# The two later layer norms of a fused attention, state-space and feed-forward kernel: constant in the root's bias, rows normalised, turned and copied in two halves

## The chip, the cores and the metric

One core of a Trainium2 chip runs the whole program in one launch. The metric is the device time of one execution in microseconds (us), lower is better. The engines are PE (TensorE, matmuls and transposes), DVE (VectorE), ACT (ScalarE), POOL (GpSimd) and SP (SyncE, which here only issues transfers). Each runs its own queue in order, and they meet in semaphores.

## What is computed

The input x has 128 rows of 512 numbers, the context 2048 rows of 512. The reference ends in three residual steps:

```
x = x + cross_attention(layernorm(x), ctx, Wq, Wk, Wv, Wo)        # 32 heads, 4 key/value heads
x = x + mamba2(layernorm(x), in_proj, conv, dt_bias, A_log, D, norm_w, out_proj)
x = x + sparse_ffn(layernorm(x), c1, c2, w1, w2)
layernorm(x) = (x - mean(x)) / sqrt(var(x) + 1e-5)                 # over the 512 numbers of a row
```

The second and third layer norm are the ones that the change touches. The first stays as it is.

## The kernel before

The 128 rows lie on the 128 partitions. `res` [128, 512] holds x and takes each residual. The three steps of the reference are three stages that follow one another without overlap in their main data: attention from about 10 to 363 us of the profiled span, the state-space stage from 367 to 586, the feed-forward stage from 590 to the end. Between two stages stands a layer norm, and nothing of the next stage can start before it, since every product reads its result.

A layer norm passes work between three engines. DVE (`norm(k)`) computes statistics of `res` (`bn_stats`, `bn_aggr` into `mean_var`), adds the constant EPS to the variance, ACT (`norm_sqrt`) takes the root, DVE takes the reciprocal and writes `normed` = (res - mean) * rstd over all 512 columns. PE (`norm_transpose`) turns four 128x128 blocks of `normed` into one PSUM bank, bank 7, and ACT (`norm_evac`) copies that bank into `norm_t` [128, 4, 128]. One semaphore, `ln`, counts these 8 steps; each step waits for the count of the one before it. Ahead of the turns PE runs 12 products of the identity (WARM) into bank 5, which nobody reads.

What stands behind each of the two norms:

- Behind the second norm (k = 1), PE makes the product with `w_dt` (4 steps c over 128 rows of the contraction, line 1769) and then the first projections (`in_proj`, line 1780, a loop over 8 chunks of weights, each 16 products). ACT, behind `norm_evac(1, 7)`, takes an exponential (line 891), which needs another function table than the root. DVE, behind `norm(1)`, fills `upper`, reduces five small selector tiles from the identity (`pick`), waits for the product with `w_dt`, and computes the step sizes in a chain of small operations that ends in `a_rows` (line 1296). PE reads `a_rows` in `cumulate` (line 1789), behind the third projection chunk.
- Behind the third norm (k = 2), PE makes the product with `c1` (line 1896) from `norm_t`, then a first product of the feed-forward with `norm_hi` (line 1904), then a product with c2 (line 1925) and the rest of the feed-forward. ACT makes `norm_hi`, the rounded upper part, from bank 7 right behind `norm_evac`; DVE makes `norm_lo` = bank 7 - `norm_hi`.

The order on every engine is written out by hand; there is no planner. Weights stream through a ring of six 1 MB slots that SP fills as PE frees them. The same ACT queue holds, ahead of the second norm's root, the last copy of the attention stage (`o_split(1)`, line 884), and the tables were last set for the exponential of the softmax.

Of the kernel before, what the change touches and what calls it, by code (L numbers as in the profile page):

```python
# [18 lines left out]
F32 = mybir.dt.float32  # L19
F32R = mybir.dt.float32r  # L20
I32 = mybir.dt.int32
ALU = mybir.AluOpType
ACT = mybir.ActivationFunctionType
# [3 lines left out]
P = 128  # L27
T = 128
DM = 512
NC = DM // P  # L30
BANK = 512
EPS = 1e-5
# [52 lines left out]
LN_STEPS = 8  # L85
# [48 lines left out]
def build(nc, x, ctx_t, wq, wk, wv, wo, w_in, w_dt, w_out, conv_w, conv_b, dt_bias, a_log, d_skip,  # L134
          norm_w, c1, c2, w1, w2, w2_tail, out):
    with ExitStack() as ctx:
        def sem(name):
            return ctx.enter_context(nc.semaphore(name))

        def sbuf(stack, name, shape, dt=F32):  # L140
            return stack.enter_context(nc.sbuf_tensor(name, shape, dt))
# [16 lines left out]
        res = sbuf(ctx, "res", [P, DM])  # L158
        normed = sbuf(ctx, "normed", [P, DM])
        norm_t = sbuf(ctx, "norm_t", [P, NC, T])  # L160
        ident = sbuf(ctx, "ident", [P, P])
        stats = sbuf(ctx, "stats", [P, 6])
        mean_var = sbuf(ctx, "mean_var", [P, 2])
        rstd = sbuf(ctx, "rstd", [P, 3])
        row_inv = sbuf(ctx, "row_inv", [P, 2, 2])
        o_hi = sbuf(ctx, "o_hi", [P, 2 * P], F32R)
        o_lo = sbuf(ctx, "o_lo", [P, 2 * P], F32R)
# [45 lines left out]
        with ExitStack() as st3:  # L213
# [27 lines left out]
            with ExitStack() as st4:  # L241
# [5 lines left out]
                with ExitStack() as st5:  # L247
# [4 lines left out]
                    norm_hi = sbuf(st5, "norm_hi", [P, NC, T], F32R)  # L252
                    norm_lo = sbuf(st5, "norm_lo", [P, NC, T], F32R)
# [20 lines left out]
                with ExitStack() as same_place:  # L274
# [7 lines left out]
        ps = ctx.enter_context(nc.psum_tensor("ps", [P, 8, BANK], F32))  # L282
# [10 lines left out]
        ident_ok = sem("ident_ok")  # L293
        pool_const = sem("pool_const")
        ln = sem("ln")
        first_in = [sem(f"first_in{c}") for c in range(NC - 1)]
        first_hi, first_ctx, first_lo = sem("first_hi"), sem("first_ctx"), sem("first_lo")
        w_hi, w_lo, c_hi, c_lo = sem("w_hi"), sem("w_lo"), sem("c_hi"), sem("c_lo")
# [25 lines left out]
        w1_in, w1h_ok, w1l_ok, nh_ok, nl_ok = (sem("w1_in"), sem("w1h_ok"), sem("w1l_ok"), sem("nh_ok"),  # L324
                                               sem("nl_ok"))
# [72 lines left out]
        def wo_home(m):  # L398

            late = isinstance(m, int) and m >= LAST_PAIR - 1  # L400
            return half(ring[0 if late else 1], m % 2).rearrange("p (h n) -> p h n", h=2)
# [6 lines left out]
        def half(tile, m):  # L408

            return tile[:, (m % 2) * 2 * DM:(m % 2 + 1) * 2 * DM]  # L410

        block = ctx.enter_context(nc.Block())

# [124 lines left out]
        def _(pool):  # L538
# [2 lines left out]
            pool.affine_select(out=ident[:], in_=ident[:], compare_op=ALU.not_equal, fill=1.0, base=0,  # L541
                               pattern=[[-1, P]], channel_multiplier=1).then_inc(ident_ok, 1)
            pool.wait_ge(ident_ok, 2)

            sub = lambda dst, a, hi: pool.tensor_tensor(dst, a, hi, ALU.subtract)  # L545

# [25 lines left out]
            for n in range(LAST_PAIR - 1):  # L572
                kv, p = n // PAIRS, n % PAIRS
# [79 lines left out]
        def _(act):  # L653
            copy = lambda dst, src: nc.scalar.activation(dst, src, ACT.Copy)  # L654

            def norm_sqrt(k):
                act.wait_ge(ln, LN_STEPS * k + 3)
                nc.scalar.activation(rstd[:, 1:2], rstd[:, 0:1], ACT.Sqrt).then_inc(ln, 1)

            def norm_evac(k, bank):  # L660
                act.wait_ge(ln, LN_STEPS * k + 7)
                copy(norm_t[:], ps[:, bank, :].rearrange("p (c t) -> p c t", c=NC)).then_inc(ln, 1)
# [221 lines left out]
            o_split(1)  # L884


            norm_sqrt(1)
            norm_evac(1, 7)

            act.wait_ge(dts, 2)  # L890
            nc.scalar.activation(softplus[2][:], softplus[1][:], ACT.Exp, scale=-1.0).then_inc(dts, 1)
# [107 lines left out]
            nc.scalar.activation(rstd[:, 1:2], rstd[:, 0:1], ACT.Sqrt).then_inc(var_s, 1)  # L999


            norm_sqrt(2)
            norm_evac(2, 7)
            copy(norm_hi[:], ps[:, 7, :].rearrange("p (c t) -> p c t", c=NC)).then_inc(nh_ok, 1)
            act.wait_ge(r1_ps, 1)
            copy(r1_st[:], ps[0:STACK, 6, 0:T]).then_inc(r1h_ok, 1)
            for i in range(4):
# [7 lines left out]
        def _(dve):  # L1015
            sub = lambda dst, a, hi: nc.vector.tensor_tensor(dst, a, hi, ALU.subtract)

            def norm(k):

                nc.vector.bn_stats(stats[:], res[:]).then_inc(ln, 1)  # L1020
                dve.wait_ge(ln, LN_STEPS * k + 1)
                nc.vector.bn_aggr(mean_var[:], stats[:]).then_inc(ln, 1)
                dve.wait_ge(ln, LN_STEPS * k + 2)
                nc.vector.tensor_scalar(rstd[:, 0:1], mean_var[:, 1:2], EPS, None, ALU.add).then_inc(ln, 1)
                dve.wait_ge(ln, LN_STEPS * k + 4)
                nc.vector.reciprocal(rstd[:, 2:3], rstd[:, 1:2]).then_inc(ln, 1)
                dve.wait_ge(ln, LN_STEPS * k + 5)
                nc.vector.tensor_scalar(normed[:], res[:], mean_var[:, 0:1], rstd[:, 2:3],
                                        ALU.subtract, ALU.mult).then_inc(ln, 1)

            def split_first(c):
                if c < NC - 1:
                    dve.wait_ge(first_in[c], 32)
                else:
                    dve.wait_ge(landed[2], 16)
                nc.vector.tensor_copy(ctx_hi[0][:, c, :], ring[2][:, c * DM:(c + 1) * DM]).then_inc(first_ctx, 1)
                dve.wait_ge(first_hi, c + 1)
                sub(wk_lo[:, c, :], ring[0][:, c * DM:(c + 1) * DM],
                    wk_hi[:, c, :].bitcast(F32)).then_inc(first_lo, 1)
                dve.wait_ge(first_ctx, c + 1)  # L1040
                sub(ctx_lo[0][:, c, :], ring[2][:, c * DM:(c + 1) * DM],
                    ctx_hi[0][:, c, :].bitcast(F32)).then_inc(first_lo, 1)

            def split_wv():
                dve.wait_ge(w_hi, 1)
                sub(wv_lo[:], ring[1][:].rearrange("p (c n) -> p c n", c=NC),
                    wv_hi[:].bitcast(F32)).then_inc(w_lo, 1)
                dve.wait_ge(w_lo, 1)
                dve.sem_inc(freed[1], 1)
# [22 lines left out]
            for c in range(NC):  # L1072
                split_first(c)
# [170 lines left out]


            dve.wait_ge(wo_ev, 2 * PAIRS_ALL)
            norm(1)
            dve.wait_ge(pool_const, 4)
            nc.vector.tensor_scalar(upper[0:64, :], causal[0:64, :], -1.0, None, ALU.add).then_inc(pool_const, 1)
            nc.vector.tensor_copy(upper[64:P, :], causal[64:P, :]).then_inc(pool_const, 1)  # L1250
# [29 lines left out]
            k = 8  # L1280
# [118 lines left out]
            def w1_split(c):  # L1399
# [29 lines left out]
            dve.wait_ge(res_ok, 1)  # L1429


            norm(2)
            nc.vector.tensor_copy(rank[:], rank_i[:]).then_inc(pool_const, 1)
            dve.wait_ge(nh_ok, 1)
            sub(norm_lo[:], ps[:, 7, :].rearrange("p (c t) -> p c t", c=NC),
                norm_hi[:].bitcast(F32)).then_inc(nl_ok, 1)
            dve.wait_ge(r1h_ok, 1)
            sub(r1_st[32:32 + RANK, :], ps[32:32 + RANK, 6, 0:T],
                r1_st[32:32 + RANK, :].bitcast(F32)).then_inc(r1l_ok, 1)
# [1 line left out]
            for i in range(4):  # L1441
# [3 lines left out]
                k, top, first = key[:, n0:n0 + n, :], bmax[:, n0:n0 + n], kmax[:, n0:n0 + n]  # L1445
# [22 lines left out]
        def _(pe):  # L1468
            mm = nc.tensor.matmul

            def norm_transpose(k, bank):
                pe.wait_ge(ln, LN_STEPS * k + 6)
                for c in range(NC):
                    ins = nc.tensor.transpose(ps[:, bank, c * P:c * P + P], normed[:, c * P:c * P + P], ident[:])
                ins.then_inc(ln, 1)

            def split_product(dst, a_hi_, a_lo_, b_hi_, b_lo_, first, last):

                mm(dst, a_hi_, b_hi_, start=first, stop=False)  # L1479
                mm(dst, a_lo_, b_hi_, start=False, stop=False)  # L1480
                return mm(dst, a_hi_, b_lo_, start=False, stop=last)  # L1481
# [79 lines left out]
            for c in range(NC):  # L1561
                ins = split_product(ps[:, 0, :], lat_hi[:, c, :], lat_lo[:, c, :], wk_hi[:, c, :], wk_lo[:, c, :],
                                    c == 0, c == NC - 1)
# [5 lines left out]
            for kv in range(KVH):  # L1569
                ins = nc.tensor.transpose(ps[:, 4, kv * P:kv * P + P], normed[:, kv * P:kv * P + P], ident[:])  # L1570
# [178 lines left out]
            for c in range(NC):  # L1749
                ins = split_product(ps[:, 4, :], lat_hi[:, c, :], lat_lo[:, c, :], wv_hi[:, c, :], wv_lo[:, c, :],  # L1750
                                    c == 0, c == NC - 1)
# [8 lines left out]

            for _ in range(WARM):
                mm(ps[:, 5, 0:P], ident[:], ident[:], start=True, stop=True)
            norm_transpose(1, 7)


            pe.wait_ge(ln, 2 * LN_STEPS)
            pe.wait_ge(const_in, 128)
            for c in range(NC):
                ins = mm(ps[:, 6, 0:NH], norm_t[:, c, :], w_dt_sb[:, c, :], start=(c == 0), stop=(c == NC - 1))
            ins.then_inc(dt_ps, 1)  # L1770

# [78 lines left out]
            for g in range(GROUPS):  # L1850
                ins = mm(ps[:, 6 + g // 4, (g % 4) * T:(g % 4 + 1) * T], bc[:, g, :], bc[:, 8 + g, :],
                         start=True, stop=True)
# [36 lines left out]

            for _ in range(WARM):  # L1890
                mm(ps[:, 5, 0:P], ident[:], ident[:], start=True, stop=True)
            norm_transpose(2, 7)
            pe.wait_ge(ln, 3 * LN_STEPS)
            pe.wait_ge(stack_in, 96)
            for c in range(NC):
                ins = mm(ps[0:STACK, 6, 0:T], c1_sb[:, c, :], norm_t[:, c, :], start=(c == 0), stop=(c == NC - 1))
            ins.then_inc(r1_ps, 1)

# [35 lines left out]
            for i in range(4):  # L1934
# [5 lines left out]
                for t in range(4 * i, min(4 * i + 4, NFT)):  # L1940
                    ins = mm(ps[:, 4, :], hsel_t[:, t, :], ring[s][:, (t % 4) * DM:(t % 4 + 1) * DM],  # L1941
                             start=(t == 0), stop=(t == NFT - 1))
# [59 lines left out]
```

## Time and profile before

| | |
|---|---|
| median of 3 runs | 621.16 us (620.96 to 621.83) |
| the profiled execution | 620.81 us |
| its span, first to last instruction | 619.1 us |
| granted TensorE clock over the span | 1.000 |
| PE busy | 607.1 us, 98% of the span |
| DVE, ACT, POOL busy | 430.3, 349.5, 206.2 us |

The profile gives, of one execution, the busy time of each engine and the chain of work that ended last: starting from the last instruction, at each step what released it. The 1.7 us between span and execution time lie outside the first and last instruction. "issue" in the chain is time in which an engine waited for nothing that the profile shows. A letter q behind an engine (ACTq, DVEq) is the queue's own instruction, such as a wait that stands by itself.

### The profile page before, as it was taken

The page shows a single profiled execution, that of the slowest core. Times are in us where ns is not written, and L with a number is a line of the kernel's source. Part 1 is how long each engine was busy: PE and PEld are TensorE (multiplying, and loading weights), DVE is VectorE, ACT ScalarE, POOL GpSimd, SP SyncE. Part 2 cuts the span into 40 slices and gives each one's busy share as a digit, 9 for nine tenths or more (in the row PEclk, how much of TensorE's full clock was granted, in tenths as well). Part 3 has the DMA queues.
Part 4 walks back from the last instruction along what each step waited for, and adds up shares of the span by engine and source line. Part 5 has one row for each costly group of instructions (what it writes and reads, how often), then busy time and mean ns, then how long its engine had stood idle before and what let it go on. Part 6 is the DMA issues. An engine that isn't in the chain of part 4 may idle for free.

```text
span 619.1 us, 10957 instructions
## 1 busy us (share of the span) xinstructions
PE 607.1 (98%) x3892; PEld 520.6 (84%) x3892; DVE 430.3 (70%) x887; ACT 349.5 (56%) x630; POOL 206.2 (33%) x164
## 2 busy tenths in 40 slices
PE   8999999999999999999999989999999999999997
PEld 7888888799898999899988989998879779787573
DVE  4533137678888888888886767989683674858773
ACT  2513115668676767777776636697565474466110
POOL 0000002259778877887786712114000000000000
PEclk9999999999999999999999999999999999999999
DMA  8600011878887888887777939476766867788400
GB/s 263 230 1 32 3 35 39 215 189 215 213 214 200 205 213 213 213 212 191 202 179 190 336 138 258 181 279 250 287 230 247 281 215 278 251 368 323 189 1 17
DMA packets 29536, 120.66 MB, mean 195 GB/s; under 512 B 7680, under 2 KB 8064, under 8 KB 21936
## 3 DMA queue, kind: packets, MB, share of 16 engines
q1 hardware_dynamic: 28912, 118.96, 62.3%
q10 hardware_dynamic: 576, 1.05, 0.6%
q8 instruction: 31, 0.51, 0.3%
q14 instruction: 17, 0.14, 0.1%
HBM read 86.30 MB, written 0.26 MB: 140 GB/s over the span
## 4 chain that ended last, share of the span: by engine, by line
PE 82%; POOL 6%; DVE 5%; issue 2%; ACT 2%; DMA 1%; DVEq 0%; SPq 0%; ACTq 0%
PE ps L1780 21%; PE ps L1479 11%; PE ps L1481 11%; PE ps L1480 11%; PE ps L1831 9%; PE ps L1580 4%; POOL pt_lo L545 3%; PE ps L1656 3%; PE ps L1820 2%; PE ps L1941 2%; PE ps L1540 2%; POOL v_lo L545 2%; PE ps L1904 2%; DVE prob_far L1116 2%; DMA ring<-wk_dram 1%
## 5 line engine op out<-in xcount | busy, mean ns | idle before, releaser
L1780 PEld LDWEIGHTS ps<-norm_t,ring 128*128 128x128 f32 x1152 | 131.7, 192 | 4.8 <-issue 4.1
L1780 PE MATMUL ps<-norm_t,ring 128*128 128x128 f32 x1152 | 133.4, 276 | 0.0
L545 POOL TENSOR_TENSOR pt_lo<-far_t,pt_hi 128x512 fp32r<-128x512 f32 (+1 forms) x94 | 111.8, 1213 | 54.7 <-ACT pt_hi L654 54.3
L728 ACT ACTIVATE prob_far<-prob_far,neg_max 128x1024 f32<-128x1024 f32 (+2 forms) x96 | 85.5, 892 | 55.1 <-DVE neg_max L1120 55.1
L1116 DVE TENSOR_SCALAR_CACHE_REDUCE prob_far<-ps 128x256 f32<-128x256 f32 (+2 forms) x96 | 86.7, 906 | 31.9 <-PE ps L1481 31.5
L1140 DVE STREAM_TRANSPOSE prob_far<-prob_far 128x2176 f32<-128x2176 f32 x30 | 73.1, 2437 | 0.8 <-ACT prob_far L728 0.2
L1306 DVE SCALAR_TENSOR_TENSOR acc<-raw,cw,acc 128x127 f32<-128x127 f32 (+2 forms) x240 | 65.7, 348 | 9.2 <-ACT acc L905 8.6
L1479 PE MATMUL ps<-pt_hi,v_hi 128*128 128x256 f32 x208 | 61.1, 294 | 2.8 <-POOL pt_lo L545 2.3
L1479 PE MATMUL ps<-k_hi,q_hi 128*128 128x512 f32 (+2 forms) x160 | 61.4, 384 | 1.4 <-ACT v_all L654 0.7
L1481 PE MATMUL ps<-pt_lo,v_hi 128*128 128x256 f32 x208 | 58.8, 283 | 0.0
L1480 PE MATMUL ps<-pt_hi,v_lo 128*128 128x256 f32 x208 | 58.7, 282 | 0.0
L654 ACT ACTIVATE pt_hi<-far_t 128x512 fp32r<-128x512 f32 (+1 forms) x105 | 57.8, 589 | 0.9 <-PE ps L1481 0.5
L1480 PE MATMUL ps<-k_hi,q_lo 128*128 128x512 f32 (+2 forms) x160 | 57.7, 361 | 0.0
L1481 PE MATMUL ps<-k_lo,q_hi 128*128 128x512 f32 (+2 forms) x160 | 57.3, 358 | 0.0
L1831 PE MATMUL ps<-ring,ug 128*128 128x512 f32 x128 | 56.7, 594 | 0.0
L545 POOL TENSOR_TENSOR v_lo<-v_all,v_hi 128x256 fp32r<-128x256 f32 (+2 forms) x12 | 16.6, 1390 | 105.5 <-ACT v_hi L654 105.5
L1831 PEld LDWEIGHTS ps<-ring,ug 128*128 128x128 f32 x128 | 23.5, 190 | 26.7 <-issue 26.0
L1479 PEld LDWEIGHTS ps<-pt_hi,v_hi 128*128 128x128 f32 x208 | 39.5, 190 | 6.2 <-POOL pt_lo L545 3.9
L1480 PEld LDWEIGHTS ps<-pt_hi,v_lo 128*128 128x128 f32 x208 | 39.5, 190 | 1.1
L1481 PEld LDWEIGHTS ps<-pt_lo,v_hi 128*128 128x128 f32 x208 | 39.4, 189 | 0.0
L545 POOL TENSOR_TENSOR wo_lo<-ring,wo_hi 128x1024 fp32r<-128x1024 f32 x15 | 37.4, 2492 | 0.0
L1479 PEld LDWEIGHTS ps<-k_hi,q_hi 128*128 128x128 f32 x160 | 30.3, 189 | 6.9 <-DVE prob_far L1116 1.6
(227 smaller groups left out, 1116.2 us busy)
## 6 DMA issues: line engine op xcount, KB each, us to landing
ring<-w_in_dram SPq DMA_DIRECT2D x36, 1024.0 KB, 5.0
far_t<-prob_far SPq DMA_DIRECT2D x240, 136.0 KB, 2.6
ring<-w_out_dram SPq DMA_DIRECT2D x16, 1024.0 KB, 4.8
ring<-wq_dram SPq DMA_DIRECT2D x16, 512.0 KB, 4.1
ring<-wo_dram SPq DMA_DIRECT2D x16, 512.0 KB, 3.9
w_sb<-w_dram SPq DMA_DIRECT2D x4, 896.0 KB, 9.8
ring<-ctx_t_dram SPq DMA_DIRECT2D x3, 1024.0 KB, 5.9
ring<-w_dram SPq DMA_DIRECT2D x3, 1024.0 KB, 9.2
```

The lines of the kernel that those rows point to most:

```text
L545: sub = lambda dst, a, hi: pool.tensor_tensor(dst, a, hi, ALU.subtract)
L654: copy = lambda dst, src: nc.scalar.activation(dst, src, ACT.Copy)
L728: nc.scalar.activation(tile, tile, ACT.Exp, bias=neg_max[:, b, h:h + 1], accum_out=part_sum[:, b, h, i:i + 1]).then_inc(exp_ok, 1)
L1116: nc.vector.tensor_scalar(piece_prob(m, b, h, i), piece_ps(m, h, i), SCALE, None, ALU.mult, ALU.max, accum_out=chunk_max[:, b, h, i:i + 1] ...
L1140: nc.vector.transpose(blocks, blocks).then_inc(turned, 1)
L1306: ins = nc.vector.scalar_tensor_tensor(a[:, i, back:], r[:, i, 0:T - back], cw[:, bass.ds(tile + i, 1), 3 - back:4 - back].rearrange("p a ...
L1479: mm(dst, a_hi_, b_hi_, start=first, stop=False)
L1480: mm(dst, a_lo_, b_hi_, start=False, stop=False)
L1481: return mm(dst, a_hi_, b_lo_, start=False, stop=last)
L1580: ins = mm(ps[:, bank, h * P:h * P + P], w[:, c, h * P:h * P + P], norm_t[:, c, :], start=(c == 0), stop=(c == NC - 1))
L1780: ins = mm(ps[:, bank, t * T:t * T + T], w[:, t, c, :], norm_t[:, c, :], start=(c == 0), stop=(c == NC - 1))
L1831: ins = mm(ps[:, 6, :], ug[b][:, 4 * i + t, :], w[:, t, :], start=(first and i == 0 and t == 0), stop=(last and i == 1 and t == 3))
```

## The change

A new column `eps_col` holds EPS, set by POOL at the very start behind the identity. The layer norms k = 1 and k = 2 become:

- DVE's addition of EPS goes away; ACT's root reads the variance directly and adds `eps_col` as its bias. In the text, the root now waits for two semaphores, `eps_ok` first and `mid` second.
- DVE writes `normed` in two halves of 256 columns, each with its own count.
- PE turns blocks 0 and 1 into bank 5 and blocks 2 and 3 into bank 7, each pair when its half is there.
- ACT copies the left pair from bank 5, DVE the right pair from bank 7, each half into its part of `norm_t`. The products with w_dt and with c1 wait for the left half at c = 0 and for the right at c = 2.
- Behind the third norm, `norm_hi` and `norm_lo` are made from `norm_t`, not from PSUM, and `norm_hi` waits for both halves.

```
+            pool.memset(eps_col[:], EPS).then_inc(eps_ok, 1)
...
-            norm_sqrt(1)
-            norm_evac(1, 7)
+            def half_norm(k):
+
+                act.wait_ge(eps_ok, 1)
+                act.wait_ge(mid, 3 * k - 1)
+                nc.scalar.activation(rstd[:, 1:2], mean_var[:, 1:2], ACT.Sqrt, bias=eps_col[:, 0:1]).then_inc(root_ok, 1)
+                act.wait_ge(half_ps, 2 * k - 1)
+                copy(norm_t[:, 0:2, :], turned_half(0).rearrange("p (c t) -> p c t", c=2)).then_inc(left_half, 1)
+
+            half_norm(1)
...
-            norm_sqrt(2)
-            norm_evac(2, 7)
-            copy(norm_hi[:], ps[:, 7, :].rearrange("p (c t) -> p c t", c=NC)).then_inc(nh_ok, 1)
+            half_norm(2)
+            act.wait_ge(right_half, 2)
+            act.wait_ge(left_half, 2)
+            copy(norm_hi[:], norm_t[:]).then_inc(nh_ok, 1)
...
+            def half_norm(k):
+
+                nc.vector.bn_stats(stats[:], res[:]).then_inc(mid, 1)
+                dve.wait_ge(mid, 3 * k - 2)
+                nc.vector.bn_aggr(mean_var[:], stats[:]).then_inc(mid, 1)
+                dve.wait_ge(root_ok, k)
+                nc.vector.reciprocal(rstd[:, 2:3], rstd[:, 1:2]).then_inc(mid, 1)
+                dve.wait_ge(mid, 3 * k)
+                for h in range(2):
+                    cols = slice(2 * P * h, 2 * P * h + 2 * P)
+                    nc.vector.tensor_scalar(normed[:, cols], res[:, cols], mean_var[:, 0:1], rstd[:, 2:3],
+                                            ALU.subtract, ALU.mult).then_inc(half_ok, 1)
+
+            def right_out(k):
+
+                dve.wait_ge(half_ps, 2 * k)
+                nc.vector.tensor_copy(norm_t[:, 2:4, :],
+                                      turned_half(1).rearrange("p (c t) -> p c t", c=2)).then_inc(right_half, 1)
...
-            norm(1)
+            half_norm(1)
+            right_out(1)
...
-            norm(2)
+            half_norm(2)
+            right_out(2)
...
-            sub(norm_lo[:], ps[:, 7, :].rearrange("p (c t) -> p c t", c=NC),
-                norm_hi[:].bitcast(F32)).then_inc(nl_ok, 1)
+            sub(norm_lo[:], norm_t[:], norm_hi[:].bitcast(F32)).then_inc(nl_ok, 1)
...
+            def half_turns(k):
+
+                for h in range(2):
+                    pe.wait_ge(half_ok, 2 * k - 1 + h)
+                    for c in range(2):
+                        at = (2 * h + c) * P
+                        ins = nc.tensor.transpose(turned_half(h)[:, c * P:c * P + P], normed[:, at:at + P], ident[:])
+                    ins.then_inc(half_ps, 1)
...
-            norm_transpose(1, 7)
-            pe.wait_ge(ln, 2 * LN_STEPS)
+            half_turns(1)
+            pe.wait_ge(left_half, 1)
             pe.wait_ge(const_in, 128)
             for c in range(NC):
+                if c == 2:
+                    pe.wait_ge(right_half, 1)
                 ins = mm(ps[:, 6, 0:NH], norm_t[:, c, :], w_dt_sb[:, c, :], start=(c == 0), stop=(c == NC - 1))
```

Behind the third norm PE's code changes in the same way, with `c1_sb`. `turned_half(h)` is `ps[:, 5 + 2 * h, 0:256]`.

## Rows read from the trace of the kernel before

**Rows 1.** The page: shares of the chain that ended last, by engine.

```profile
PE 82%; POOL 6%; DVE 5%; issue 2%; ACT 2%; DMA 1%; DVEq 0%; SPq 0%; ACTq 0%
```

**Rows 2.** The chain through the second norm: start us, us, what.

```profile
364.21 0.20 DVE mean_var L1022
...
364.43 0.17 DVE rstd L1024
...
364.62 0.21 ACT rstd L658
...
365.05 0.56 DVE normed L1028
...
365.65 0.67 PE ps L1474 x4
...
366.35 0.61 ACT norm_t L654
...
367.00 1.16 PE ps L1769 x8
```

**Rows 3.** The chain from the last residual of the state-space stage through the third norm.

```profile
586.19 0.02 DVEq L1426
...
586.25 0.76 DVE res L1427
...
587.77 0.20 DVE mean_var L1022
...
588.61 0.56 DVE normed L1028
...
590.55 1.10 PE ps L1896 x8
591.65 0.93 PE ps L1904 x4
```

**Rows 4.** Timeline of ACT at two table loads: start, us, engine, line, operation [idle before].

```profile
360.72 1.28 ACT L658 ACT_TABLE_LOAD   x1
...
401.75 1.28 ACT L925 ACT_TABLE_LOAD   x1
403.05 1.06 ACT L925 ACTIVATE decay<-decay 128x1024 f32<-128x1024 f32 x1
```

**Rows 5.** Line 929, the second of two waits: ns min/median/max, first and last start.

```profile
L929 ACTq EVENT_SEMAPHORE  x8: 17/17/17, 418.6 to 569.0; - x8
```

**Rows 6.** Groups of DVE by form: busy us, mean ns of one, idle before.

```profile
L1028 DVE TENSOR_SCALAR normed<-res,mean_var,rstd 128x512 f32<-128x512 f32 x3 | 1.6, 546 | 0.1
...
L1092 DVE COPY normed<-ps 128x512 f32<-128x512 f32 x1 | 0.7, 692 | 0.9 <-PE ps L1481 0.9
...
L1296 DVE COPY a_rows<-a_f 128x512 f32<-128x512 f32 x1 | 0.4, 427 | 0.0
...
L1449 DVE TENSOR_TENSOR key<-ps,bmax 128x256 f32<-128x256 f32 x1 | 0.4, 425 | 0.0
```

**Rows 7.** Groups of ACT by form.

```profile
L905 ACT ACTIVATE acc<-ps,cb,cw 128x128 f32<-128x128 f32 x80 | 30.0, 462 | 0.0
...
L654 ACT ACTIVATE lat_hi<-norm_t 128x512 fp32r<-128x512 f32 x1 | 0.6, 632 | 0.0
...
L654 ACT ACTIVATE hsel_t<-ps 128x256 f32<-128x256 f32 x1 | 0.4, 384 | 3.1 <-PE ps L1914 3.1
...
L654 ACT ACTIVATE r_st<-ps 80x128 fp32r<-80x128 f32 x1 | 0.3, 273 | 0.7 <-PE ps L1896 0.7
```

**Rows 8.** Timeline of PE's weight loads behind the third norm.

```profile
591.38 0.77 PEld L1904 LDWEIGHTS ps<-w_hi,norm_hi 128*128 128x128 f32 x4
```

**Rows 9.** Timeline of DVE at the end of the step sizes.

```profile
374.88 0.43 DVE L1296 COPY a_rows<-a_f 128x512 f32<-128x512 f32 x1
```

**Rows 10.** The chain where PE reads `a_rows`.

```profile
378.88 0.89 PE ps L1789 x8
```

**Rows 11.** Waits of the state-space stage: us in total, times, longest.

```profile
DVE gm L1367 <- PE ps L1851: 2.9, 1, 2.9
...
DVE softplus L1267 <- PE ps L1769: 1.3, 1, 1.3
```

More of the change, by code:

```diff
@@ L164, in build @@
         rstd = sbuf(ctx, "rstd", [P, 3])
+        eps_col = sbuf(ctx, "eps_col", [P, 1])
         row_inv = sbuf(ctx, "row_inv", [P, 2, 2])
@@ L295, in build @@
         ln = sem("ln")
+        eps_ok, mid, root_ok, half_ok, half_ps, left_half, right_half = (
+            sem("eps_ok"), sem("mid"), sem("root_ok"), sem("half_ok"), sem("half_ps"), sem("left_half"),
+            sem("right_half"))
         first_in = [sem(f"first_in{c}") for c in range(NC - 1)]
@@ L410, in half, with turned_half @@
             return tile[:, (m % 2) * 2 * DM:(m % 2 + 1) * 2 * DM]
+        def turned_half(h):
+            return ps[:, 5 + 2 * h, 0:2 * P]
         block = ctx.enter_context(nc.Block())
@@ L1891, in _ @@
                 mm(ps[:, 5, 0:P], ident[:], ident[:], start=True, stop=True)
-            norm_transpose(2, 7)
-            pe.wait_ge(ln, 3 * LN_STEPS)
+            half_turns(2)
+            pe.wait_ge(left_half, 2)
             pe.wait_ge(stack_in, 96)
             for c in range(NC):
+                if c == 2:
+                    pe.wait_ge(right_half, 2)
                 ins = mm(ps[0:STACK, 6, 0:T], c1_sb[:, c, :], norm_t[:, c, :], start=(c == 0), stop=(c == NC - 1))
```

## The prediction

> **What bounds the kernel now.** I read the chain first. Four fifths of it is PE [rows 1], and inside the stages PE never stops, so the time is PE's own work plus the few places where PE has nothing it may do. The two layer norms that the change touches are two of these places. The chain zoomed to each of them gives the whole hand-over from engine to engine: [rows 2] for the second norm, [rows 3] for the third. The reader is to see there that no step has slack: each starts 0.02 to 0.04 us behind the end of the one before it. So a step shortened here comes off the end, as long as PE is the bound behind it, and a step lengthened is paid in full. Then I read ACT's timeline for its table loads [rows 4], the queue's own waits [rows 5], and the groups by form for what each new operation costs [rows 6, 7].
>
> **The halves.** I count from the start of `normed`. Before, it takes 0.60 to PE's first turn, and PE starts the next product at 367.00 - 365.05 = 1.95 us [rows 2].
>
> A half of `normed` is a form the trace lacks. A copy of 512 columns takes 427 ns and `normed` 546 [rows 6]. The same columns cost 119 ns more with two pointer operands, which I take as fixed. A one-column operation of DVE lasts some 0.16 (the `rstd` piece in [rows 2] is 0.17), so 427 is about 0.16 fixed and 0.27 for 512 columns. A half is 546 - 133 = 413 ns. If all but 0.16 of the 546 went with the columns, it would be 0.35; that is the lower end. Two independent operations in a row overlap a little in this trace (I take 0.08). The first half ends at 0.41, the second at 0.74, later than the whole did at 0.56.
>
> Turns: four take 0.67 and the eight matmuls behind them 1.16 [rows 2], so each further one costs (1.16 - 0.67) / 4 = 0.12 and a pair takes 0.67 - 0.24 = 0.43. The left pair runs from 0.45 to 0.88, the right from 0.78 to 1.21.
>
> Copies: ACT's copy of 256 columns out of PSUM takes 384 ns [rows 7], so the left half is there at 0.90 + 0.38 = 1.29, and PE starts at 1.33. DVE's copy of 512 columns out of PSUM takes 692 and an operation of 256 with a PSUM operand 425 [rows 6], so the right half is there at 1.23 + 0.43 = 1.66, seen by PE at 1.69. PE wants it at c = 2, four matmuls after 1.33, which is 1.82. So PE doesn't stop there, with 0.13 to spare. The gain of the halves is 1.95 - 1.33 = 0.62 us in each norm. Bounds: 0.68 with the lower price of a half, and about 0.4 if the operations on 256 columns and the waits come out a tenth dearer and the margin at c = 2 goes.
>
> **The constant.** Taken away is DVE's addition with its hand-over, 364.62 - 364.41 = 0.21 us [rows 2]; what remains of the hand-over is 0.02. Added are two things. The root now has a bias read by pointer. The nearest row: an activation of 128 columns with bias and scale by pointer takes 462 ns, a copy of 128 columns 273 [rows 7]; half the difference, 0.095, for one pointer. And it now has two waits. Where two waits stand, the trace has the last written one as an event of its own in the queue (line 929 is the second wait of `squares`, and line 928, the first, has no row [rows 5]); the first rides on the instruction. At line 1426, again the second wait, the instruction starts 0.06 behind that event's start [rows 3]. So the wait for `mid`, which is the one that comes late, is the separate one, and costs 0.06. From the end of `mean_var` to the start of `normed` it was 0.21 + 0.43 = 0.64 us [rows 2]; it becomes 0.02 + 0.06 + 0.43 + 0.095 = 0.605. The constant alone brings 0.03 us. Bounds: 0.19 if neither pointer nor wait cost anything, a loss of 0.05 if both cost half as much again.
>
> **The table load.** This is the point that decides. In the second norm the root needs another table than ACT has. Before, the load stands at 360.72 [rows 4] and the root starts at 364.62 [rows 2]: the load ran while ACT had nothing to do, because the root's only wait rides on the root and not ahead of the load. The load has the line of its activation, so it belongs directly to it. With the wait for `mid` now a separate event ahead of the root, the load can stand ahead of this event (hidden as before) or between event and root. In the second case 1.28 us and a hand-over of 0.02 [rows 4] fall onto the chain. No row shows the order of the two. I take the second case, since a load tied to its activation has no reason to be put ahead of a foreign event. The Trainium skill, "ScalarE: Activation LUTs", section "What happens when an `exp` ACTIVATE runs", says that the compiler places the load right before the ACTIVATE, which is my case; that it did so here no row shows. In the third norm the root of line 999 has just run, so its table is there and nothing is loaded.
>
> The second norm then: `mean_var` ends 364.41, the event passes and the load starts at 364.49, ends 365.77; the root starts 365.79, `normed` 0.43 + 0.095 later at 366.315, PE at 366.315 + 1.33 = 367.645. Before, 367.00: **0.65 us later**. With the load hidden: 364.49 + 0.525 + 1.33 = 366.345, 0.66 earlier.
>
> **The third norm.** `normed` starts at 587.97 + 0.605 = 588.575 and PE's product with c1 at 589.905, 0.645 earlier than 590.55 [rows 3]. But `norm_hi` now waits for both halves: 588.575 + 1.66 + 0.02 = 590.255, and reads 512 columns from SBUF, 632 ns [rows 7], until 590.89; PE sees it at 590.93. PE had loaded the first weights with `norm_hi` at 591.38 [rows 8], 0.83 behind the start of c1, so it would be ready at 590.74 and now waits 0.19. What is left is 591.40 - 590.93, **0.47 us earlier**. Behind it DVE makes `norm_lo` and the low part of the stack while PE has 0.93 us of `norm_hi` products [rows 3]; this stays hidden by about 0.1 us, which bounds the loss.
>
> **What else moves.** DVE's queue in the second norm now holds `right_out` ahead of `upper` and the picks. They start at 366.315 + 1.66 = 367.97 and not at 365.61, 2.36 later, of which 1.3 was waiting for the product with w_dt anyway [rows 11]. So the step sizes come 1.06 later. `a_rows` was ready at 375.31 [rows 9], PE reads it at 378.88 [rows 10]: 2.9 us of slack even without PE's own 0.65. The convolutions are 0.4 later against PE, and DVE later waits 2.9 us for the gm product [rows 11], where it catches up. Cost: nothing. With that cover gone it would be 0.4. POOL's memset runs at the start behind the identity, far ahead of use. PE stands idle 1.3 us longer before the turns; the granted clock is 1.000 over the whole span, through an idle stretch of 0.7 ahead of the product with w_dt [rows 2], and I take it unchanged.
>
> **Sum.** +0.65 - 0.47 = +0.18 us. The profiled execution took 620.81 (span 619.1), which gives 620.99; the median shown lies 0.35 above that execution, so 621.16 + 0.18 = **621.3 us**.
>
> **Rivals.** First, the load stays ahead of the wait: -0.66 - 0.47 = -1.13 us, 620.0. For it: all loads before run ahead of their waits [rows 2, 4]; against it: those waits ride on the activation. Second, on the slow side: the load behind the wait costs more than its own 1.28, since the activation behind it is held. The place is the root of the second norm; the rows give 0.02 from load to activation when nothing else is awaited [rows 4]. It decides (over 0.2%, 1.24 us) from 1.06 us of extra. At another full load's length, 1.28 [rows 4], the sum is +1.46, 622.6. The skill, same page, section "What ACT_TABLE_LOAD costs", gives a drain of about 1.38 us beside each load, 2.66 in all; by it, as an estimate, the sum would be +1.56, 622.7. This trace shows 1.30 from load to activation, and disagrees. Third, the halves gain little, 0.3 instead of 0.62 (PE stops at c = 2 for DVE's copy, or the second half of `normed` holds up the turns): the load behind the wait, and 0.3 less in either norm, gives +0.8, 622.0.
>
> **Chances and range.** The likeliest case 0.68, the hidden load 0.17, the held activation 0.06, weak halves 0.07, else 0.02. Within 0.2% (1.24 us, about what a measurement of this kernel can tell from no change) lie nearly all of the first, two thirds of the second, as its -1.13 is just inside, and most of the weak halves. So same 0.78, faster 0.12, slower 0.10. The likeliest case's own range is 620.7 to 621.9, its bounds of 0.3 up and down with the spread of the runs. The range of 8 in 10 takes in the hidden load and some of the weak halves: 619.9 to 622.1.
>
> **What would show it.** Right: ACT's table load at line of the root starts at about 364.5 and not at 360.7, the root at 365.8 with 0.30 us, `normed` as two of 0.41, the product with w_dt at about 367.6; in the third norm the product with c1 0.65 earlier, then a gap of PE of about 0.2 ahead of the `norm_hi` products. The stretch between the norms stays 215 us with no wait of PE for DVE. Wrong: a load still at 360.7 (first rival); more than 0.1 us between load and root (second); an idle gap of PE inside the w_dt or c1 products (third).

## Result and the profile after

The changed kernel takes 622.23 us (median of 18 runs, 620.88 to 624.02) against 621.02 for the kernel before (18 runs, 620.48 to 621.90): a ratio of 1.0020, interval 1.0014 to 1.0027. It is slower by 1.2 us, where 0.2 was forecast. A second comparison, the experiment "The changed kernel again" below, gave 1.0017 (1.0008 to 1.0026).

The runs of the changed kernel fall into two groups by their mean granted TensorE clock. Eleven of 18 have 0.999 or 1.000 and a median of 621.91 us; seven have 0.997 and a median of 623.53. No run of the kernel before is under 0.999 in the comparisons for which its clocks were listed (62 runs). The profiled execution (624.02 us, span 622.3) is of the second group.

The chain of the changed kernel through the second norm (start us, us, what), against [rows 2]:

```profile
364.71 0.71 DVE stats L1063
...
365.44 0.20 DVE mean_var L1065
...
365.65 0.02 ACTq L899
...
365.70 1.28 ACT L900
...
366.99 0.30 ACT rstd L900
...
367.52 0.42 DVE normed L1071
...
367.99 0.46 PE ps L1520 x2
...
368.46 0.39 ACT norm_t L663
...
368.90 1.29 PE ps L1817 x8
```

Read it from the third line. `ACTq L899` is the wait for `mid` as an event of its own, released as `mean_var` ends. Behind it, and no longer ahead of it, stands the table load of line 900 with its whole 1.28 us. In [rows 4] the same load ran at 360.72, four microseconds before anybody wanted the root. From the end of `mean_var` to the start of `normed` it is now 1.89 us and was 0.64 [rows 2]; from `normed` to the w_dt product it is 1.38 and was 1.95.

The chain through the third norm, against [rows 3]:

```profile
589.79 0.76 DVE res L1464
...
591.31 0.19 DVE mean_var L1065
...
591.52 0.02 ACTq L899
...
591.58 0.30 ACT rstd L900
...
592.11 0.42 DVE normed L1071
...
593.49 1.10 PE ps L1946 x8
594.59 1.12 PE ps L1954 x4
595.71 0.41 PE ps L1975
```

The same separate wait, but no load, since the table is there. The piece of line 1954 is 1.12 and was 0.93 [rows 3]: the 0.19 is PE's wait for `norm_hi`.

What the forecast did not have is in the granted clock. The windows of the changed kernel around the turns (us; busy time and count of PE, PEld, DVE, ACT, POOL; PEclk, DMA share, GB/s):

```profile
366.00:368.00 2.00, 0.32 (x4) 0.13 (x3) 0.65 (x3) 1.27 (x2) 0.00 (x0) 1.00 0.00 0
368.00:369.00 1.00, 0.84 (x5) 0.49 (x5) 0.47 (x2) 0.52 (x2) 0.00 (x0) 1.00 0.00 0
369.00:370.00 1.00, 1.00 (x9) 1.00 (x10) 0.94 (x5) 1.00 (x1) 0.00 (x0) 0.90 0.00 0
370.00:371.00 1.00, 1.00 (x6) 1.00 (x6) 0.96 (x7) 0.15 (x1) 0.00 (x0) 0.50 0.00 0
371.00:372.00 1.00, 1.00 (x7) 1.00 (x6) 0.59 (x3) 0.51 (x2) 0.00 (x0) 0.50 0.00 0
372.00:373.00 1.00, 1.00 (x7) 1.00 (x7) 0.93 (x3) 0.00 (x0) 0.00 (x0) 0.50 0.00 0
373.00:374.00 1.00, 1.00 (x10) 1.00 (x10) 0.90 (x4) 0.00 (x0) 0.00 (x0) 0.90 0.00 0
374.00:375.00 1.00, 1.00 (x12) 1.00 (x11) 0.90 (x4) 0.00 (x0) 0.00 (x0) 1.00 0.00 0
```

PE is busy 0.32 us of the first two; the turns start at 367.99, and some 1.8 us later the clock is at 0.50, that is 1.2 instead of 2.4 GHz, for some 3.4 us (0.50 in three windows, and the 0.90 of the windows on either side stands for 0.2 us each). There PE makes 6 or 7 matmuls in a microsecond where it makes 12 at full clock. And PE's own view of the gap:

```profile
367.99 0.76 PE L1520 MATMUL ps<-ident,normed 128*128 128x128 f32 x4 [1.68 <-DVE normed L1071]
```

PE stood idle 1.68 us ahead of the turns. Before, it was 0.56:

```profile
365.65 0.66 PE L1474 MATMUL ps<-ident,normed 128*128 128x128 f32 x4 [0.56 <-DVE normed L1028]
```

The account of the two profiled executions, from four stretches of their chains, with those of the experiments that follow (us; the last column is the start of the statistics of the second norm):

| kernel | statistics to w_dt | w_dt to `res` | `res` to c1 | c1 to c2 product | start |
|---|---|---|---|---|---|
| before | 3.52 | 219.25 | 4.30 | 2.03 | 363.48 |
| changed | 4.19 | 220.89 | 3.70 | 2.22 | 364.71 |
| changed again | 4.20 | 220.89 | 3.70 | 2.23 | 363.54 |
| waits exchanged | 2.85 | 219.25 | 3.64 | 2.23 | 364.14 |
| more identity products | 4.19 | 219.24 | 3.70 | 2.22 | 364.67 |
| load late, nothing else | 4.85 | 220.86 | 4.30 | 2.03 | 364.23 |
| waits exchanged, `norm_hi` in halves | 2.85 | 219.27 | 3.64 | 2.03 | 363.96 |
| constant alone | 3.41 | 219.29 | 4.20 | 2.03 | 364.55 |
| halves alone | 2.95 | 219.27 | 3.74 | 2.22 | 364.20 |
| fewer identity products | 3.83 | 221.79 | 4.30 | 2.02 | 363.72 |

Before to changed: +0.67, +1.64, -0.60, +0.19, and +1.23 in the start. The start is not the change's: the changed kernel itself has 364.71 in one profile and 363.54 in another. The chain shows where, in the landing of the first weights, before and changed:

```profile
1.27 8.49 DMA ring<-wk_dram
```

```profile
1.27 9.64 DMA ring<-wk_dram
```

The landing is 1.15 us longer in this execution of the changed kernel, nearly all of the 1.23. It differs from one execution to the next, also where nothing of the change is in the kernel (9.33 us in the experiment of the late load).

### The profile page after: what moved, and what is told of

Same layout as the page of the kernel before. It is cut to its first block, busy times and chain, and to the rows that moved or that the text cites. A ratio compares the mean times of both kernels' runs of the same rounds, so it can differ in the third digit from the quotient of the medians.

```text
span 622.3 us, 10962 instructions
## 1 busy us (share of the span) xinstructions
PE 608.9 (98%) x3892; PEld 521.7 (84%) x3892; DVE 430.3 (69%) x889; ACT 349.3 (56%) x630; POOL 206.0 (33%) x165
## 4 chain that ended last, share of the span: by engine, by line
PE 82%; POOL 6%; DVE 5%; ACT 2%; issue 2%; DMA 2%; DVEq 0%; SPq 0%; ACTq 0%
PE ps L1828 21%; PE ps L1525 11%; PE ps L1526 10%; PE ps L1527 10%; PE ps L1879 9%; PE ps L1626 4%; POOL pt_lo L554 3%; PE ps L1702 2%; PE ps L1868 2%; PE ps L1991 2%; PE ps L1586 2%; POOL v_lo L554 2%; PE ps L1954 2%; DMA ring<-wk_dram 2%; DVE prob_far L1152 2%
## 5 line engine op out<-in xcount | busy, mean ns | idle before, releaser
L1828 PEld LDWEIGHTS ps<-norm_t,ring 128*128 128x128 f32 x1152 | 133.3, 194 | 4.8 <-issue 4.1
L1828 PE MATMUL ps<-norm_t,ring 128*128 128x128 f32 x1152 | 134.9, 277 | 0.0
```

Source lines behind the costliest of these rows:

```text
L1828: ins = mm(ps[:, bank, t * T:t * T + T], w[:, t, c, :], norm_t[:, c, :], start=(c == 0), stop=(c == NC - 1))
```

## Experiments

Each ran in five rounds beside the kernel before, the first four on one chip (before: 621.30 us, 29 runs), the others on another (before: 621.62, 33 runs).

**The two waits exchanged.**

```
             def half_norm(k):
-                act.wait_ge(eps_ok, 1)
                 act.wait_ge(mid, 3 * k - 1)
+                act.wait_ge(eps_ok, 1)
```

> The changed kernel with the two waits of the root exchanged in the text, mid first and eps_ok second. My theory: the wait written first rides on the root, so the table load stands ahead of it again and runs at about 362, right behind the last attention copy. The w_dt product starts 3.52 - 0.09 - 0.57 = 2.86 us behind the start of the statistics (before 3.52, changed 4.19), the TensorE clock stays at 1.000 in every run, and the time is that of before less 1.1 us (ratio 0.998). Rival, that the load goes behind the wait whatever the order: nothing changes against the changed kernel, ratio 1.002 and a clock of 0.997 in about 7 of 18 runs.

Measured: 620.43 us, ratio 0.9981 (0.9972 to 0.9990), all eleven runs at 0.999 or 1.000. ACT's timeline of this kernel:

```profile
361.37 1.28 ACT L900 ACT_TABLE_LOAD   x1
365.08 0.29 ACT L900 ACTIVATE rstd<-mean_var,eps_col 128x1 f32<-128x1 f32 x1 [2.43 <-DVE mean_var L1065]
```

The load is back in ACT's idle time, at 361.37, and the root waits for `mean_var` itself. Every engine does the same work as in the changed kernel; only the order of two waits differs, of which one has been satisfied since the start of the program. The time is 0.87 us under before, where 1.1 was expected; the chain holds 1.13. Between the ratios, 0.9981 here and 1.0020 and 1.0017 for the changed kernel, lie 2.2 to 2.4 us. The chains hold 1.34 of it for the load and 0.06 for the third norm; the rest I put down to the clock and the spread of the runs, which this experiment doesn't separate. The rival, that the load goes behind the wait in either order, is out.

**More products of the identity**, so that PE is busy while it waits.

```
-            for _ in range(WARM):
+            for _ in range(WARM + 6):
                 mm(ps[:, 5, 0:P], ident[:], ident[:], start=True, stop=True)
             half_turns(1)
```

> The changed kernel with 18 products of the identity ahead of the turns of the second norm instead of 12, which fill 1.4 of the 1.68 us in which TensorE now stands idle; the table load stays where it is. My theory: the lower clock of some runs follows from that idle stretch, so here every run has a clock of 1.000, the first projections take 10.7 us for 96 matmuls, and the time is that of before plus 0.67 - 0.43 = 0.24 us (ratio 1.0004), with no runs above 622.5. Rival, that the lower clock comes from elsewhere (the halves, chance of the chip): it stays in about 7 of 18 runs and the ratio is 1.002.

Measured: 621.59 us, ratio 1.0003 (0.9994 to 1.0012), no run under 0.999, the highest 622.37. In its profile PE stands idle 0.34 us ahead of the turns, and behind them the clock stays up:

```profile
368.00:372.00 4.00, 3.85 (x32) 3.49 (x33) 2.96 (x13) 2.18 (x4) 0.00 (x0) 1.00 0.00 0
```

The late load is still there (4.19 in the table), and w_dt to `res` takes 219.24. So the 1.64 us of the middle are the clock's. What is left without them, +0.67 - 0.60 + 0.19 = +0.26, agrees with the time (+0.29), though the interval is 0.6 us wide on either side.

**The load late, in the kernel before.**

```
             def norm_sqrt(k):
+                if k == 1:
+                    act.wait_ge(ident_ok, 2)
                 act.wait_ge(ln, LN_STEPS * k + 3)
```

> The kernel before with one more wait, always satisfied, written ahead of the wait of the second norm's root, and nothing else. My theory: the wait for ln becomes a separate event and the table load falls between it and the root: w_dt starts 3.52 + 1.34 = 4.86 us behind the statistics. TensorE stands idle 1.9 us ahead of the turns and the clock falls afterwards in at least as many runs as with the change, costing 1.5 us each time: plus 1.35 us in the good runs, plus 2.9 in the others, median ratio about 1.003. Rival, that the lower clock belongs to the halves: clock 1.000 in all runs and exactly plus 1.35 us.

Measured: 623.70 us, ratio 1.0038 (1.0024 to 1.0052), six runs, clocks 1.000, 0.999, 0.999, 0.997, 0.997, 0.995. Its chain:

```profile
365.36 0.02 ACTq L659
...
365.41 1.28 ACT L660
...
366.70 0.21 ACT rstd L660
```

One wait that is always satisfied, written ahead of the real one, moves the load onto the chain and costs 1.33 us in the norm, with neither halves nor a bias. The lower clock comes with it in half of the runs: the three at 0.999 or 1.000 have a median of 622.79, 1.49 above before, the three others 624.49, 3.19 above, with few runs in either group. The rival, that the clock belongs to the halves, is out.

**Fewer products of the identity, in the kernel before.**

```
-            for _ in range(WARM):
+            for _ in range(WARM - 6):
                 mm(ps[:, 5, 0:P], ident[:], ident[:], start=True, stop=True)
             norm_transpose(1, 7)
```

> The kernel before with 6 products of the identity ahead of the turns of the second norm instead of 12, and nothing else. No step of the norm is later; TensorE only stands idle 1.98 us ahead of the turns instead of 0.56. My theory, that the idle stretch by itself brings the lower clock: some runs have a clock of 0.997 and lie 1.5 us above the others, as with the changed kernel, where the stretch is 1.68 us; the others take the time of before. Rival, that the lower clock needs something of the changed kernel or of the late load: clock 1.000 in all runs and the time of before, ratio 1.000.

Measured: 622.51 us, ratio 1.0009 (0.9999 to 1.0019), which by itself says little. The runs say more: five at 1.000 with a median of 621.37, six at 0.997 or 0.994 with a median of 622.85, 1.5 us above. The profiled one is the longest:

```profile
362.48 1.50 PE L1762 MATMUL ps<-ident 128*128 128x128 f32 x12
365.89 0.97 PE L1474 MATMUL ps<-ident,normed 128*128 128x128 f32 x4 [1.91 <-DVE normed L1028]
367.55 1.86 PE L1769 MATMUL ps<-w_dt_sb,norm_t 128*128 128x128 f32 x7 [0.69 <-ACT norm_t L654]
```

```profile
366.00:368.00 2.00, 1.31 (x6) 0.91 (x7) 1.10 (x6) 1.09 (x2) 0.00 (x0) 0.52 0.03 8
368.00:372.00 4.00, 4.00 (x21) 4.00 (x21) 1.87 (x5) 1.30 (x3) 0.00 (x0) 0.50 0.00 0
372.00:376.00 4.00, 4.00 (x34) 4.00 (x34) 3.57 (x13) 1.15 (x3) 0.00 (x0) 0.89 0.13 16
```

Up to `normed` no step of the norm is later than before; PE is only left idle 1.91 us instead of 0.56, by leaving out work that nobody reads. Its turns take 0.97 and the clock is at 0.50 through 368 to 372. In this profile the clock is down almost as soon as the turns start (0.52 over 366 to 368), and the mean of 0.994 is that of this run alone; the five others of the lower group have 0.997. An idle stretch of this length is enough to bring the lower clock in some executions, and whether it does is not the kernel's to say: same kernel, same chip.

**The parts alone.** The constant alone is `half_norm` with the wait for `mid` first, one `normed` of 512 columns, four turns into bank 7, one copy. The halves alone are the changed kernel with the addition put back:

```
             def half_norm(k):

-                act.wait_ge(eps_ok, 1)
-                act.wait_ge(mid, 3 * k - 1)
-                nc.scalar.activation(rstd[:, 1:2], mean_var[:, 1:2], ACT.Sqrt, bias=eps_col[:, 0:1]).then_inc(root_ok, 1)
+                act.wait_ge(mid, 4 * k - 1)
+                nc.scalar.activation(rstd[:, 1:2], rstd[:, 0:1], ACT.Sqrt).then_inc(root_ok, 1)
```

> The kernel before with the constant as the root's bias in both later norms (the wait for mid written first, so the table load stays hidden), and no halves: one normalisation, four turns into bank 7, one copy by ScalarE. My theory: 0.21 us of the addition go, 0.09 come for the pointer and 0.02 for the hand-over, 0.095 us less per norm: before less 0.19 us, ratio 0.9997. Rival: the whole 0.21 comes off, or a bias by pointer costs as much as the addition: less 0.4 or nothing.

> The changed kernel with VectorE's addition of EPS put back, so that the root has one wait and no bias: the halves alone. My theory: from normed to the w_dt product 1.38 us and not 1.95, from normed to the first norm_hi product 0.40 less: before less 0.97 us, ratio 0.9984, clock 1.000 in all runs. Rival, that part of the loss of the changed kernel belongs to the halves: a ratio of 1.000 or above, or a clock under 1.000 in some runs.

Measured: the constant alone 621.19 us, ratio 0.9993 (0.9984 to 1.0002), not told apart from no change by its time; in the chain it takes 0.11 and 0.10 us out of the two norms. The halves alone 620.92 us, ratio 0.9989 (0.9980 to 0.9998), all clocks at 0.999 or 1.000; in the chain -0.57 and -0.56 + 0.19, a sum of -0.94. The halves are sound, and none of the loss is theirs.

**The changed kernel again.** No edit.

> The changed kernel once more, on the chip of the three others. My theory: two groups of runs, one with a clock of 1.000 at before plus 0.25 us, one with 0.997 another 1.5 us above it; the median between them by chance. Rival, that a part of the difference is neither the late load nor the clock: the group with a clock of 1.000 lies 0.8 us or more above before.

Measured: 622.59 us, ratio 1.0017 (1.0008 to 1.0026). Six of eleven runs at 0.999 or 1.000 have a median of 621.79, 0.17 above before; five at 0.997 have 622.96, another 1.2 above. Here the good group lies where the forecast put it, and the rest is the clock. In its profile PE stands idle 1.66 us ahead of the turns, and the clock is down behind them again:

```profile
368.00:372.00 4.00, 4.00 (x23) 4.00 (x23) 3.15 (x13) 1.49 (x3) 0.00 (x0) 0.58 0.00 0
```

**`norm_hi` in halves from PSUM**, on top of the exchanged waits.

```
-            act.wait_ge(right_half, 2)
-            act.wait_ge(left_half, 2)
-            copy(norm_hi[:], norm_t[:]).then_inc(nh_ok, 1)
+            copy(norm_hi[:, 0:2, :], turned_half(0).rearrange("p (c t) -> p c t", c=2))
+            act.wait_ge(right_half, 2)
+            copy(norm_hi[:, 2:4, :], turned_half(1).rearrange("p (c t) -> p c t", c=2)).then_inc(nh_ok, 1)
```

> The kernel of the exchanged waits, and norm_hi of the third norm made in two halves out of PSUM by ScalarE, the left right behind its copy of the left half, the right behind the copy of VectorE. My theory: TensorE waits 0.17 us less for norm_hi, because the second half ends 0.25 us earlier than the whole did: before less 1.3 us. Rival: the wait only moves to the c1 product or the low part, and the time is that of the kernel of the exchanged waits, before less 1.1.

Measured: 620.12 us, ratio 0.9983 (0.9974 to 0.9992). The chain of this kernel behind the third norm:

```profile
589.72 1.10 PE ps L1946 x8
590.82 0.93 PE ps L1954 x4
591.75 0.94 PE ps L1975 x4
```

The piece of line 1954 is back at 0.93, so PE's wait for `norm_hi` is gone, 0.20 us (c1 to the c2 product takes 2.03 and not 2.23). The times of the two versions, 620.12 and 620.43, can't be told apart by their intervals. This kernel beats the one before, by its interval, and the changed one, whose interval lies above 1.

## Why the prediction was wrong

**What held.** That the later-written wait becomes a separate event and the table load falls behind it was the case taken as likeliest, and the trace shows it. Second norm: +0.65 forecast, +0.67 measured. Third norm: -0.47 forecast, -0.60 + 0.19 = -0.41 measured (the sum used 591.40 for the start of the first `norm_hi` weights, where the row has 591.38 [rows 8]; with it the forecast is -0.45). `normed` to the product: 1.33 forecast, 1.38 measured. A half of `normed` 0.413 forecast, 0.409 measured. The root 0.30 with its pointer, as forecast. PE's wait for `norm_hi` 0.19 forecast and measured. The load was followed by the root within 0.01 us, so the second rival, the held activation, is out. The Trainium skill, "ScalarE: Activation LUTs", section "What ACT_TABLE_LOAD costs", gives a drain of about 1.38 us beside each load. The trace disagrees: 0.01 us lie between this load and the root, and ahead of the next load, at 368.87, 0.03 us behind the end of the copy before it. The Trainium skill, same page, section "Step-by-step: what each stage is for", states that the compiler places the load right before the ACTIVATE that needs it. The trace agrees, with the load at 365.70 and its root at 366.99. The late `right_out` cost nothing: with the clock at full rate the stretch behind the second norm takes 219.24 to 219.29 us in every version.

**The step that failed** is in "what else moves": "PE stands idle 1.3 us longer before the turns; the granted clock is 1.000 over the whole span, through an idle stretch of 0.7 ahead of the product with w_dt [rows 2], and I take it unchanged." The row it rested on was of a stretch of 0.7 us and said nothing of one of 1.7. The idle stretch itself grew by 1.12, from 0.56 to 1.68, not by 1.3. What came of it was put at nothing and cost 1.64 us from w_dt to `res` in the profiled execution. In 12 of 29 runs of the changed kernel the mean clock is the lower one, and at the median these runs take 1.62 us more than the others in the first comparison and 1.18 in the second. The two of the 12 that were profiled both have the drop behind that stretch; for the other ten the place is not shown. Products of the identity that leave 0.56 us idle with the norm of the old length leave 1.68 with the new. The forecast counted the length that the load adds and did not ask what else had been sized by it.

**What stays open.** In the first comparison the eleven runs at 0.999 or 1.000 lie 0.89 us above the runs before, in the second six lie 0.17 above. The chains hold 0.26. So the clock doesn't account for the whole miss in the first comparison: the median of all 18 runs is only 0.32 above that of the eleven, and it is these 0.32 that carry it over the forecast's upper end of 622.1. The other 0.6 us or so stay open. In the second comparison the clock accounts for nearly all, 622.59 against 621.79. The landing of the first weights, which varied by over 1 us between profiled executions, is large enough for the rest (the execution profiled with more identity products, at full clock, has the landing at 9.69 us and takes 622.37), but that it made the difference between the medians was not shown. It is also not shown what decides, from one execution to the next, whether the clock falls.

## What to carry to other kernels

When an instruction has two waits and needs another function table, write the wait that comes late first. In every version traced here the first wait rode on the instruction and left the load in the idle time ahead of it, while a wait written second was an event of its own with the load behind it, and where that wait was the late one it cost 1.33 to 1.34 us. And when a step ahead of TensorE gets longer, ask what TensorE was kept busy with meanwhile, and lengthen that too: with six more unread products all eleven runs kept the clock, and the stretch from the statistics to the w_dt product stayed at 4.19 us. Look at the granted clock of every run, not only of the profiled one; a median over two groups of runs is a mixture.

## What was not expected of the hardware

An idle stretch of 1.66 to 1.91 us on TensorE went with the lower mean clock in 12 of 29 runs of the changed kernel, in 6 of 11 with fewer identity products and in 3 of 6 with the late load alone. The four of these 21 runs that were profiled all have the drop at this place of the program. Where the stretch ahead of the turns was 0.56 us or less and the longest around them 0.69, no run did so: 62 runs of the kernel before and 55 of the experiments.

The clock didn't fall in the idle stretch but behind it, while TensorE was busy again, and not at a fixed distance. Counted from the start of the turns it fell after some 0.2 us with fewer identity products, 1.2 and 1.8 in the two profiles of the changed kernel, and 2.3 with the late load. It stayed down for some 3.4 us in three of the profiles and 6.8 in that of the fewer products. (These times are worked out from windows of 1 us.) In the first profile of the changed kernel it cost 0.13 us in the w_dt product and 1.50 over the first 96 projection matmuls, which took, before and changed:

```profile
368.16 10.72 PE ps L1780 x96
```

```profile
370.19 12.22 PE ps L1828 x96
```
